# Attention with a fused mixture: ScalarE's rescaling factors, the row sums, the row splits and two weight splits issued one step sooner, on one Trainium2 core

## The reference, cut to what matters

```python
x = x + layernorm(attention(layernorm(x), wq, bq, wk, bk, wv, bv, wo, bo))
x = x + layernorm(ffn(layernorm(x), ...))

# attention, B=2, S=2048, D=1024, 16 heads of 64, causal
q, k, v = x @ wq.T + bq, x @ wk.T + bk, x @ wv.T + bv
scores = einsum('bqhd,bkhd->bhqk', q, k) / 8
scores = where(causal, -inf, scores)
attn = einsum('bhqk,bkhd->bqhd', softmax(scores), v) @ wo.T + bo
```

## Time and profile before

| | |
|---|---|
| Median of 3 runs | 2613.95 us (2604.55 to 2616.06) |
| The profiled execution's own time | 2613.59 us |
| Its span in the trace | 2611.8 us |
| PE busy | 2291.2 us (88%) |
| DVE, ACT, POOL busy | 1701.4, 1726.7, 1682.1 us (65%, 66%, 64%) |
| DMA queue q1, share of 16 engines' span | 90.8% |

### The profile page before, as it was taken

One profiled execution on the slowest core, in us unless ns is written; L12 is line 12 of the kernel. 1 busy time (PEld: TensorE's weight loads), 2 busy tenths in 40 slices (PEclk: granted clock), 3 DMA queues, 4 the chain that ended last, 5 costly groups with the idle time before them and its releaser, 6 DMA issues. The chain is left out here.

```text
span 2611.8 us, 70598 instructions
## 1 busy us (share of the span) xinstructions
PE 2291.2 (88%) x28626; PEld 1449.2 (55%) x28626; DVE 1701.4 (65%) x4154; ACT 1726.7 (66%) x2355; POOL 1682.1 (64%) x1295
## 2 busy tenths in 40 slices
PE   4899898989899888898998999999998449999995
PEld 2466656565656556556565657574756234544443
DVE  8576677676776655566566665666665554777776
ACT  3467677667676666666767677676766664666665
POOL 4577877778777776677777777777777662222221
PEclk9999999999999999999999999999999779999997
DMA  9699999999999999999999999898999985666662
GB/s 233 137 184 188 187 191 186 187 182 179 197 182 178 183 177 195 196 174 173 166 167 173 162 168 168 161 177 160 172 162 161 204 173 121 162 162 162 162 161 81
DMA packets 1424676, 450.05 MB, mean 172 GB/s; under 512 B 1402048, under 2 KB 1402448, under 8 KB 1424352
## 3 DMA queue, kind: packets, MB, share of 16 engines
q1 hardware_dynamic: 1424352, 445.54, 90.8%
HBM read 67.95 MB, written 41.94 MB: 42 GB/s over the span
## 5 line engine op out<-in xcount | busy, mean ns | idle before, releaser
L907 POOL TENSOR_TENSOR hl<-probs,hl 128x1024 f16<-128x1024 f32 x544 | 1194.9, 2202 | 484.3 <-ACT hl L790 479.6
L783 ACT ACTIVATE probs<-s_ps,exp_bias 128x1024 f32<-128x1024 f32 (+7 forms) x768 | 633.5, 854 | 577.8 <-DVE exp_bias L631 576.6
L626 DVE TENSOR_REDUCE neg_max<-s_ps 128x1 f32<-128x1024 f32 (+7 forms) x768 | 676.1, 905 | 77.5 <-PE s_ps L467 77.5
L790 ACT ACTIVATE hl<-probs 128x1024 f16<-128x1024 f32 x544 | 575.0, 1057 | 20.2 <-DMA pt<-hl 2.9
L467 PE MATMUL s_ps<-nat 64*128 64x512 f16 (+3 forms) x3840 | 411.6, 352 | 125.7 <-ACT probs L783 122.7
L490 PE MATMUL o_ps<-v,pt 128*128 128x65 f16 x4352 | 432.9, 194 | 79.3 <-DVE o_rows L655 69.2
L490 PEld LDWEIGHTS o_ps<-v,pt 128*128 128x128 f16 x4352 | 402.9, 97 | 117.4 <-issue 81.1
L519 PE MATMUL u_ps<-arena,w 128*128 128x512 f16 x1008 | 391.9, 389 | 77.3 <-DVE w L588 39.6
L491 PE MATMUL o_ps<-v,pt 128*128 128x65 f16 x4352 | 433.3, 195 | 0.0
L492 PE MATMUL o_ps<-v,pt 128*128 128x65 f16 x4352 | 432.3, 193 | 0.0
L491 PEld LDWEIGHTS o_ps<-v,pt 128*128 128x128 f16 x4352 | 402.1, 97 | 16.9
(11 more groups left out here) (150 smaller groups left out, 3754.3 us busy)
## 6 DMA issues: line engine op xcount, KB each, us to landing
w_raw<-in_w_pairs SPq DMA_DIRECT2D x48, 576.0 KB, 5.0
o_scratch<-o_hl SPq DMA_DIRECT2D x128, 128.0 KB, 2.7
out<-result SPq DMA_DIRECT2D x32, 512.0 KB, 3.1
x_in<-in_x SPq DMA_DIRECT2D x27, 512.0 KB, 4.7
pt<-hl SPq DMA_TRANSPOSE x544, 4.9
nat<-in_x SPq DMA_DIRECT2D x16, 512.0 KB, 4.6
xn_scratch<-xn SPq DMA_DIRECT2D x16, 512.0 KB, 3.8
xn<-in_x SPq DMA_DIRECT2D x11, 512.0 KB, 4.0
```

Source lines behind the costliest of these rows:

```text
L626: nc.vector.tensor_reduce(neg_max[:, step.round, acc, h:h + 1], s_ps[(n + h) % S_RING][:, first:end], AX_X, ALU.max, negate=True).then_inc ...
L783: last = nc.scalar.activation(probs_of(n)[:, cols], s_ps[n % S_RING][:, cols], ACT.Exp, bias=exp_bias[:, step.round, acc, h:h + 1], scale= ...
L790: nc.scalar.activation(hl_of(n, 0), probs_of(n), ACT.Copy).then_inc(p_hi_done, 1)
L907: nc.gpsimd.tensor_tensor(hl_of(n, 1), probs_of(n), hl_of(n, 0), ALU.subtract).then_inc(p_lo_done, 1)
```

## The change

```diff
-SPLITS = {"mid": {3: "q", 6: "k", 14: "v"}, "pre": {3: "q", 13: "k", 16: "v"}, "turn": {3: "q", 13: "k", 16: "v"}}
+SPLITS = {"mid": {2: "q", 5: "k", 14: "v"}, "pre": {2: "q", 13: "k", 16: "v"}, "turn": {2: "q", 13: "k", 16: "v"}}
...
         def half_done(p):
-            return first_step(p, N_ROUND // 2) + 1
+            return first_step(p, N_ROUND // 2)
...
# SyncE
                     if i == half_done(p) + 1:
                         store_rows(p, 0)
-                    if p > 0 and i == 2:
+                    if p > 0 and i == 1:
                         store_rows(p - 1, 1)
...
# VectorE
                     if evacuate:
                         output_read(*done)
+                        output_sum(*done)
+                    if opens:
+                        row_min(p, r)
                     step = step_of(p, i, kind)
                     if step:
                         row_max(*step)
-                    if evacuate:
-                        output_sum(*done)
-                    for u in units_ending(kind, i):
-                        unit_full(p + 1, u)
                     split = next_split(p, i - 1)
                     if split:
                         split_weight(*split)
-                    if opens:
-                        row_min(p, r)
+                    for u in units_ending(kind, i):
+                        unit_full(p + 1, u)
...
# ScalarE
                     if step:
                         exponentials(*step, 0)
+                    if steps_of(p)[i].opens:
+                        chunk_factors(p, steps_of(p)[i].round)
+                    if i == half_done(p) or i == 0 and p > 0:
+                        rows_high(2 * p + (0 if i else -1))
                     for u in units_ending(kind, i - 1):
                         unit_high(p + 1, u)
...
-                    if i and steps_of(p)[i - 1].opens:
-                        chunk_factors(p, steps_of(p)[i].round)
-                    if i == half_done(p) or i == 1 and p > 0:
-                        rows_high(2 * p + (-1 if i == 1 else 0))
...
# GpSimd
                     step = step_of(p, i, kind)
+                    if steps_of(p)[i].opens and (p or i):
+                        long_rows(*((p, steps_of(p)[i].round - 1) if i else (p - 1, N_ROUND - 1)))
                     if step:
                         probs_low(*step, 0)
+                    if i == half_done(p) or i == 0 and p > 0:
+                        rows_low(2 * p + (0 if i else -1))
...
-                    if steps_of(p)[i].opens and (p or i):
-                        long_rows(*((p, steps_of(p)[i].round - 1) if i else (p - 1, N_ROUND - 1)))
-                    if i == half_done(p) or i == 1 and p > 0:
-                        rows_low(2 * p + (-1 if i == 1 else 0))
```

## The result

The changed kernel takes 2501.48 us at the median (2497.45 to 2503.25, four runs), the kernel before 2613.25 on the same chip: a ratio of 0.9576, 95% interval 0.955 to 0.9601, or 112 us less where 153 were forecast. It is inside the range (2432 to 2512) and outside the likeliest case (2432 to 2490).

A forecast was written before the change was run, and what follows sets the result against it. PE was taken as the bound, idling 172.8 us over pairs 0 to 14 behind chained ACT, DVE and POOL waits. Savings of 70 + 57 + 14 = 141, plus 12 in pair 15, gave 2613.6 - 153 = 2460 us, range 2432 to 2512.

The forecast's parts named there:

- likeliest case: Whole kernel: the forecast itself, 2460 us within 2432 to 2490, chance 0.58.
- (a): Opening step: ACT's factors made there, DVE's minimum ahead of the row maxima; DVE's 172.4 us wait for the factor goes.
- (b): Opening step: POOL's row split made there too; DVE's 109.0 us wait for it before L655 goes.
- (c): DVE sums long rows ahead of the maxima: free if on time, up to 0.75 us if late; chain 5.2 to 5.4 us.
- (d): ACT makes factors and rows' high part between the two heads; 0.7 to 0.9 us charged at step 10 of each pair.
- (e): Weight q split a step sooner: PE's 39.6 + 2.9 us waits go; 0.7 us a pair kept for a long L588.
- (f): SP stores rows and loads weight k a step sooner; it waits for nothing new, count and bytes unchanged.
- 9.8 us a pair: Pair 12, steps 4, 5, 11 and 13: 2.6 + 2.9 + 2.4 + 1.9 us over, taken as all the pair's idle time.
- 70 + 57 + 14 = 141: Pairs 0 to 14: idle time saved in pairs 0 to 7, in pairs 8 to 14, and time beyond PE's idle time.
- The first: Rival: SP, busy with transposes, becomes the bound in early pairs; pairs 0 to 7 save half, 2498 us, chance 0.15.
- Tight chains: Rival: opening steps ahead of half-unit steps 0.75 us late, step 10 takes 2; 4 us a pair return, 2520 us, chance 0.12.
- ACT blocks on POOL: Rival: rows_high waits for long_rows with exponentials behind it; 5 us or more at 31 places, kernel slower, chance 0.04.

The follow-up runs named there:

- the single runs: Kernel before with one part each: factors and minimum alone 2537.53 us; row split, stores and sum alone 2554.69 us; q and k splits alone 2570.61 us.

## Why the prediction was right and wrong

**(a), (b)** were right: both waits are gone. Their worth was taken together, and the single runs show why: each alone gives 79 or 62 us while the other's wait grows.

**(c), (d)** were right in kind, and smaller than charged. Step 10 of a late pair takes 5.8 us against 5.6, so that 0.2 of the 0.7 to 0.9 us showed. The tight chain did not bind, since PE idles 0.44 us over seven pairs; the estimate of 5.4 us against 5.55 held. The sum at once did not help (2491.90 us without it).

**(e)** was right in pairs 8 to 14 about PE's wait and wrong about what it was. The 39.6 us were counted as a cost of their own, and the kernels without the new table show that (a) to (c) take nearly all of them anyway. The kernel with the old table and all else changed has no such wait of PE in its list. The 0.7 us kept for a long L588 was not spent: over the late pairs L588 took 1.217 us at the median and 1.427 at the longest.

**(f)** was called free. The stores stand ahead of the load of x, and DVE's three waits behind them are 7.7, 4.2 and 7.4 us where they were 3.7, 1.5 and 2.2 before; but putting the stores back gave only 4 us, within the intervals.

**The late pairs.** Forecast 57 us of idle time saved, measured 70.5 (71.0 less 0.44). PE's busy time fell by 10.5 us besides. The 9.8 us a pair that this began with is right as a total but not in its parts: it adds the excess length of two steps to the idle time of two others. By idle time the four steps make 9.4 us (2.3, 2.8, 2.4 and 1.9), and step 2, which was passed over (8.6 us long), has the other 0.4.

**The early pairs, the step that failed:** "I keep 3 us a pair for pairs 0 to 6 and 13 for pair 7, in all 34, and save 70". Kept were 70.8 and saved 31.0. Pair 7 kept 18.5 where 13 had been given, and hardly changed at all (139.5 us before, 139.0 now); pairs 0 to 6 kept 52.3 instead of 21. The long term of the sum was right in kind and too large, because the wait that took over was not in it: DVE's for the load of x, 46.6 us. The norm and SP had been seen as a reason to keep something, but the number had no row behind it. The row was there: before the change DVE waited 32.0 us in 10 places for x, below the cut of rows 2. With the load one step sooner PE idles 36.3 us in these pairs, and 34 had been forecast. The nearness is partly luck: pair 6 then takes 121.9 and pair 7 139.9 us and the other six at most 116.2; PE idles 11.6 us in those six, 5.0 in pair 6 and 19.8 in pair 7, where 18, 3 and 13 had been given. Written as a sum: 31.0 + 70.5 + 10.5 - 3.6 (PE's busy time in the early pairs grew) = 108.4 us, where 70 + 57 + 14 = 141 stood.

**Pair 15** gave some 7 of the 12 us: its last L655 starts 130.4 us after its beginning, 137.0 before. Its wait for the accumulator fell from 28.2 us to 4.5, but that for exponentials grew from 35.1 to 45.9 and that for transposed probabilities from 9.9 to 12.2; the changed kernel from 1909.5 to 2050:

```profile
PE s_ps L467 <- ACT probs L782: 45.9, 13, 9.9
...
PE o_ps L490 <- DMA pt<-hl: 12.2, 5, 8.0
...
PE o_ps L490 <- DVE o_rows L655: 4.5, 1, 4.5
```

**The rivals.** The first gave 2498 us, near what was measured, by half the early gain. The size was right, and so was SP as the engine, but not the mechanism: transposes of probabilities, which were to be the bound, keep up (pairs 8 to 14 need 113.3 us each with 34 of them, and PE idles 0.44 us in all). It was one small load behind them. The sign that had been named for this rival, PE waiting for `pt<-hl`, came to 7.0 us in the long stretch, all of it in pairs 6 and 7 (853.7 to 1116.2 us), beside 16.6 us for `xn_scratch`: around the turn alone the rival has a point. The likeliest case missed the measured time. The range holds it because it took in most of this rival, and that is more luck than mechanism. "Tight chains" and "ACT blocks on POOL" did not occur.

**Also lost in the early pairs:** some 2 us at step 4 of most of pairs 1 to 5. DVE in the changed kernel, pair 1:

```profile
263.71 1.22 DVE L588 SCALAR_TENSOR_TENSOR w<-w_raw,w 128x1024 f16<-128x1024 f32 x1
264.84 3.16 DVE L578 SCALAR_TENSOR_TENSOR xn<-x_in,xn 128x1024 f16<-128x1024 f32 x1
267.92 0.42 DVE L649 TENSOR_TENSOR o_part<-o_ps,factor 128x260 f32<-128x260 f32 x1
```

q's split has moved into a step that already held the norm's low part. That "step 4 kept 2 us behind a long L588" had been named as a sign of error; it is behind a long L578, whose 16 runs took 1.216 to 3.157 us. POOL at the same time:

```profile
264.73 2.19 POOL L906 TENSOR_TENSOR hl<-probs,hl 128x1024 f16<-128x1024 f32 x1 [1.16 <-ACT hl L789]
```

L578 starts 0.11 us behind that instruction and is 1.94 us longer than its shortest. The Trainium skill (SBUF — State Buffer, Who interferes with whom) says that a DVE instruction with two SBUF inputs contends with a GpSimd instruction that reads SBUF, and that the one that comes second stands until the first has released their shared ports; this row agrees with it. With the old splits and x in time step 4 lost nothing, yet later steps lost more, and the total was 6 us worse.

What stays open: how much the late sum is worth (6 to 10 us by the medians, with intervals that touch or overlap) and why, and whether the 4 us from putting the stores back are real.

## What to carry to other kernels

When engines work in strict order, a wait in the profile is a price only while nothing later on the same engine would have waited as long. Before removing the large waits, list the small ones of the engine that is to be freed (here 32 us for x) and ask of each what covered it, for the cover goes with the large wait. A small load whose consumer is due soon belongs ahead of the long transfers of a shared queue; moving it one step was worth 52 us, nearly half of what the change gave. To price several parts, run one with all the others in place, not only alone: 187 us of single gains were 112 together.

## What the runs showed of the hardware

The clock took a part that the forecast had left fixed (some 19 us that stay). The changed kernel's windows around the stall in pair 1:

```profile
320.00:334.00 14.00, 11.76 (x231) 9.84 (x228) 3.52 (x6) 7.55 (x10) 11.84 (x8) 1.00 1.16 214
334.00:345.00 11.00, 7.47 (x66) 4.29 (x67) 8.66 (x25) 5.34 (x9) 4.30 (x5) 0.53 1.04 176
345.00:359.00 14.00, 14.00 (x165) 7.94 (x164) 9.95 (x27) 10.96 (x16) 9.47 (x7) 1.00 0.82 142
```

PE's 4.49 us of waiting end at 336.25. From 334 to 345 the granted clock is 0.53, which is nearly all of those 11 us at the lower level of 1.2 GHz, and then it is full again. In pairs 8 to 14, where PE hardly waits, it is 1.00 (0.99 before the change); in pairs 0 to 7 it fell from 0.98 to 0.97 although PE idled less. With x in time it was 0.99, and the same matmuls took 18.5 us less (912.56 for 931.02); 931.02 x 0.97 / 0.99, an estimate from these rows, gives 912.2. The Trainium skill (TensorE: Matmul & The Clock Gate, HAM oscillation — how this bites in real kernels) warns that TensorE resumes at the low clock after a long wait for data; these rows agree. Whether long stalls cost more than the same time in short ones is a thing that no run here separates.
